# Stage two's rows and activations, and one key block in four of stage one, turned by VectorE and a trip through DRAM instead of TensorE

## What is computed

```python
# stage one, per block: q = layernorm(x), k = v = ctx, all [128, 1024]
qh = softmax(Wq @ q, over the 64 of a head) / 8      # 8 heads of 64
kh = softmax(Wk @ k, over the 1024 columns)
context = kh @ (Wv @ v).T                            # per head, 64 x 64
out = Wo @ (context.T @ qh) + bo
u = out / norm(out over the 128 channels) * g * sqrt(128)
x = x + tanh(g_xattn) * u
# stage two, per block: y = layernorm(x), rows of 1024
scores = y @ Wr.T                                    # 64 experts
G = softmax of the 16 largest scores, 0 elsewhere
h = y @ A.T                                          # 64 experts x rank 16 = 1024
x = x + tanh(g_ffn) * 2 * (h * G) @ B
```

## Time and profile before

| | |
|---|---|
| median of 3 runs | 959.66 us (959.61 to 959.68) |
| the profiled execution | 959.67 us, of which the span is 957.9 |
| TensorE matmuls | 932.2 us busy (97%), 5084 |
| TensorE weight loads | 800.5 us (84%) |
| VectorE | 704.0 us (73%) |
| ScalarE | 492.2 us (51%) |
| GpSimd | 469.5 us (49%) |
| DMA | 88.31 MB, mean 92 GB/s |
| granted clock | 0.994 of full |
| chain that ended last | PE 81%, DVE 10%, issue 5%, ACT, POOL and DMA 1% each |

### The profile page before, as it was taken

How to read it: one execution, slowest core, us unless ns; L and a number is a source line. 1 busy time by engine, 2 the same in 40 slices (tenths; PEclk the granted TensorE clock), 3 DMA queues, 4 the chain that set the end, 5 groups by cost and what they waited for, 6 DMA issues and landing times.

```text
span 957.9 us, 16074 instructions
## 1 busy us (share of the span) xinstructions
PE 932.2 (97%) x5084; PEld 800.5 (84%) x5084; DVE 704.0 (73%) x1532; ACT 492.2 (51%) x974; POOL 469.5 (49%) x323
## 2 busy tenths in 40 slices
PE   7899999999999999999999799999999999999998
PEld 5687887888888888888888699999999999999986
DVE  6888888888888888888888857766666666666521
ACT  4687786678768767876787634222222222222100
POOL 3775657678777877785787824222222111111100
PEclk9999999999999999999999999999999999999999
DMA  4226231231323113311312853121111111111001
GB/s 153 89 66 249 93 104 49 89 133 66 109 91 133 66 68 132 109 68 66 131 45 88 300 199 128 67 67 67 66 67 67 66 66 66 66 66 45 23 23 44
DMA packets 24805, 88.31 MB, mean 92 GB/s; under 512 B 3264, under 2 KB 3264, under 8 KB 24768
## 3 DMA queue, kind: packets, MB, share of 16 engines
q1 hardware_dynamic: 19296, 67.91, 19.9%
q0 software_dynamic: 5184, 19.40, 6.1%
q10 hardware_dynamic: 288, 0.52, 0.2%
HBM read 71.04 MB, written 16.78 MB: 92 GB/s over the span
## 4 chain that ended last, share of the span: by engine, by line
PE 81%; DVE 10%; issue 5%; ACT 1%; POOL 1%; DMA 1%; DVEq 0%; ACTq 0%; POOLq 0%
PE ps L61 22%; PE ps L63 22%; PE ps L62 22%; PE ps L1307 6%; PE ps L1298 4%; DVE qT_lo L909 3%; PE ps L1288 2%; PE ps L1402 1%; PE ps L1373 1%; DVE mt L933 1%; DVE ekT_lo L916 1%; DVE qmax L895 1%; DVE bn L831 1%; DVE kmax L889 1%; DVE qsum L900 1%
## 5 line engine op out<-in xcount | busy, mean ns | idle before, releaser
L471 POOL TENSOR_TENSOR rb<-u_in,rb 128x1024 f32<-128x1024 f32 x14 | 33.7, 2408 | 255.4 <-DVE rb L885 255.4
L400 POOL TENSOR_TENSOR qe<-qe,qrec 128x1024 f32<-128x1024 f32 x64 | 121.2, 1903 | 47.1 <-DVE qrec L903 47.1
L61 PE MATMUL ps<-aT_hi,yT_hi 128*128 128x448 f32 (+2 forms) x384 | 128.4, 334 | 5.4 <-issue 5.4
L63 PE MATMUL ps<-aT_lo,yT_hi 128*128 128x448 f32 (+2 forms) x384 | 126.6, 330 | 0.0
L62 PE MATMUL ps<-aT_hi,yT_lo 128*128 128x448 f32 (+2 forms) x384 | 126.5, 330 | 0.0
L909 DVE TENSOR_TENSOR qT_lo<-ps,qT_hi 128x512 fp32r<-128x512 f32 x128 | 82.4, 686 | 49.0 <-ACT qT_hi L628 48.5
L393 POOL TENSOR_TENSOR qhalf<-qe 128x512 f32<-128x512 f32 x64 | 82.2, 1284 | 64.8 <-ACT qe L620 61.8
L61 PE MATMUL ps<-bT_hi,hT_hi 128*128 128x512 f32 x256 | 102.6, 401 | 0.0
L63 PE MATMUL ps<-bT_lo,hT_hi 128*128 128x512 f32 x256 | 100.0, 391 | 0.0
L62 PE MATMUL ps<-bT_hi,hT_lo 128*128 128x512 f32 x256 | 99.8, 390 | 0.0
L700 ACT ACTIVATE hT_hi<-ps 128x512 fp32r<-128x512 f32 x32 | 19.1, 597 | 143.8 <-PE ps L1402 143.8
(11 more groups left out here) (155 smaller groups left out, 2397.5 us busy)
## 6 DMA issues: line engine op xcount, KB each, us to landing
x_in<-in_x SPq DMA_DIRECT2D x16, 512.0 KB, 4.4
ctx_in<-in_ctx SPq DMA_DIRECT2D x16, 512.0 KB, 4.9
ctxT_in<-in_ctxT SPq DMA_DIRECT2D x16, 512.0 KB, 3.4
ctxT_hi<-in_ctxT POOLq DMA_DIRECT2D x16, 512.0 KB, 3.8
u_scratch<-osb SPq DMA_DIRECT2D x16, 512.0 KB, 3.8
out<-res SPq DMA_DIRECT2D x16, 512.0 KB, 2.8
x<-in_x SPq DMA_DIRECT2D x15, 512.0 KB, 4.0
u_in<-u_scratch SPq DMA_DIRECT2D x14, 512.0 KB, 3.2
```

What stands on the lines that cost most here:

```text
L61: nc.tensor.matmul(psum, whi, mhi, start=start, stop=False)
L63: return nc.tensor.matmul(psum, whi, mlo, start=False, stop=stop)
L400: nc.gpsimd.tensor_tensor(v, v, w, ALU.mult).then_inc(q_norm, 1)
```

## The change

VectorE can turn 32x32 blocks in place (`nc.vector.transpose`). The rest of a 128x128 turn, the blocks' exchange, is made by a store of the tile to a DRAM scratch (`put_turned`, one DMA) and four loads of 32 partitions each, in runs of 256 elements (`take_moved`). Both are issued on SP, and SP waits for the store's end before it issues the loads.

- y of blocks 2 to 15: `turn_y` (VectorE, in place), trip, `y_raw`, then `hi_moved_y` and `lo_moved_y`, each one operation over 128x1024 from SBUF, in place of two from PSUM. `tr_y` stays for blocks 0 and 1.
- h of all 16 blocks: `turn_h` after the third `gated`, trip, `h_raw`, `hi_moved_h`, `lo_moved_h`. `down(b)` is one piece. Rows of A and B are laid out in another order to suit.
- Strip 0 of the keys in every body: `exp_k(b, 0)` writes in another order, `turn_k` follows on VectorE after `sum_q(b-1, 2)`, the trip ends in `osb`, then `hi_moved_k` (ScalarE) and `lo_moved_k` (GpSimd, after `mts`). `osb` must be free of block b-2's store, and `out_o(b-1, 0)` waits for `lo_moved_k(b)`.
- TensorE takes `tr_q(b-1, 2)` where `tr_k(b, 0)` stood; ScalarE takes `hi_q(b-1, 2)` ahead of `exp_k(b, 2)`. Stage two's `sum_u(b + 2)` moves behind `up(b, 0)`, `psN` to another bank.
- SP loads the raw A one block per body in bodies 2 to 9, not all eight ahead of body 2.

```diff
+        def put_turned(queue, place, src, s):
+            queue.dma_start(turn_dram[place], src).then_inc(s, 16)
+        def take_moved(queue, dst, place, s):
+            for q in range(P // 32):
+                queue.dma_start(dst[32 * q:32 * q + 32, :].rearrange("j (a f) -> j a f", f=256),
+                                turn_dram[place].rearrange("(a j) (q f) -> q j a f", a=P // 32, f=256)[q]).then_inc(s, 16)
...
+            def move_k(b):
+                wait_apart(sp, sp_turns, (k_turned, b + 1))
+                put_turned(sp, 2, ek[:, 0, :], k_put)
+                if not (isinstance(b, int) and b < 2):
+                    wait_apart(sp, sp_turns, (u_stored, 16 * (b - 1)))
+                wait_apart(sp, sp_turns, (k_put, PUT * (b + 1)))
+                take_moved(sp, osb, 2, k_moved)
...
                     load(ctx_in[:, :], ctx, b + 1, ctx_loaded)
+                    move_k(b)
...
+                if not isinstance(i, int) or b <= NB - 2:
+                    sp.wait_ge(y_turned, b)
+                    put_turned(sp, 0, y[(j + 2) % 2][:, :], y_put)
+                    sp.wait_ge(y_put, PUT * b)
+                    take_moved(sp, y_raw, 0, y_moved)
                 if not isinstance(i, int) or b <= NB - 4:
-                    sp.wait_ge(y_T, 2 * b + 4)
                     load_u(b + 3, j % 2)
+                sp.wait_ge(h_turned, b + 1)
+                put_turned(sp, 1, hg[:, :], h_put)
+                sp.wait_ge(h_put, PUT * (b + 1))
+                take_moved(sp, h_raw, 1, h_moved)
...
+            def lo_moved_k(b):
+                pool.wait_ge(k_hi, 8 * b + 2)
...
+            def hi_moved_k(b):
+                act.wait_ge(k_moved, MOVED * (b + 1))
...
+            def hi_moved_y(b):
+                act.wait_ge(h_mm, 3 * b)
+                act.wait_ge(y_moved, MOVED * (b - 1))
...
+            def hi_moved_h(b):
...
+                elif started(b):
+                    act.wait_ge(f_mm, 2 * b)
+                act.wait_ge(h_moved, MOVED * (b + 1))
...
                 if head:
-                    hi_k(b, 0)
+                    hi_moved_k(b)
+                if tail and head:
+                    hi_q(b - 1, 2)
+                if head:
                     exp_k(b, 2)
                     exp_q(b, 1)
-                if tail and head:
-                    hi_q(b - 1, 2)
...
                 b = SLOTS * i + j + 1
+                first = isinstance(i, int) and b == 1
+                if not first:
+                    hi_moved_h(b - 1)
                 if not isinstance(i, int) or b <= NB - 2:
                     normalise(b + 1, (j + 2) % SLOTS)
-                hi_h(b - 1, 1)
+                if first:
+                    hi_moved_h(0)
                 exp_scores(b)
                 if not isinstance(i, int) or b <= NB - 2:
-                    hi_y(b + 1)
-                hi_h(b, 0)
+                    hi_moved_y(b + 1)
...
                 if tail:
                     sum_q(b - 1, 2)
+                if head:
+                    turn_k(b)
...
                     max_q(b, 1)
                     max_k(b, 2)
-                    lo_k(b, 0)
...
-                if not (isinstance(i, int) and b < 2):
+                if not first:
                     result(b - 2, (j + 1) % 2, (j + 3) % SLOTS, 2 * i + (j - 1) // 2)
-                if not isinstance(i, int) or b <= NB - 3:
+                    lo_moved_h(b - 1)
+                if norms:
                     part_u(b + 2)
+                if ahead:
+                    turn_y(b + 1, j % 2)
                 route(b)
...
                     gated(b, p)
-                if not isinstance(i, int) or b <= NB - 2:
-                    lo_y(b + 1)
-                lo_h(b, 0)
-                if not isinstance(i, int) or b <= NB - 3:
+                turn_h(b)
+                if ahead:
+                    lo_moved_y(b + 1)
+                if norms:
                     stats2(b + 2, (j + 3) % SLOTS)
...
                 up(b, 0)
-                if isinstance(i, int) and b == 1:
-                    tr_h(0, 0)
-                else:
-                    tr_h(b - 1, 1)
+                if norms and not first:
+                    sum_u(b + 2)
                 up(b, 1)
-                if isinstance(i, int) and b == 1:
-                    tr_h(0, 1)
                 up(b, 2)
-                if not isinstance(i, int) or b <= NB - 3:
+                if first:
                     sum_u(b + 2)
-                if not isinstance(i, int) or b <= NB - 2:
-                    tr_y(b + 1, j % 2)
-                down(b - 1, 0)
-                tr_h(b, 0)
-                down(b - 1, 1)
+                down(b - 1)
```

More of the change, by code:

```diff
@@ L4, with flamingo_layer @@
 import math
-def flamingo_layer(nc, x, ctx, ctxT, g_xattn, g_ffn, WqT, WkT, Wv, WoT, bo, g, AT, BT, u_dram, out):
+def flamingo_layer(nc, x, ctx, ctxT, g_xattn, g_ffn, WqT, WkT, Wv, WoT, bo, g, AT, BT, u_dram, turn_dram, out):
     f32 = mybir.dt.float32
@@ L293, in _ @@
             sp.wait_ge(wq_low, 1)
-            for t in range(DC):
-                sp.dma_start(a_raw[:, t, :], AT[t]).then_inc(a_loaded, 16)
-            with sp.Fori(2, NB - 2) as b:
+            with sp.Fori(2, 2 + DC) as b:
+                sp.dma_start(a_raw[:, bass.ds(b - 2, 1), :].rearrange("p o n -> p (o n)"),
+                             AT[bass.ds(b - 2, 1)].rearrange("o p n -> (o p) n")).then_inc(a_loaded, 16)
+                body(b, head=True, tail=True, ahead=True)
+            with sp.Fori(2 + DC, NB - 2) as b:
                 body(b, head=True, tail=True, ahead=True)
@@ L910, in lo_q, with turn_k @@
                                             qT[0][:, :, v].bitcast(f32), ALU.subtract).then_inc(q_lo, 1)
+            def turn_k(b):
+                dve.wait_ge(k_exp, 4 * b + 1)
+                nc.vector.transpose(ek[:, 0, :], ek[:, 0, :]).then_inc(k_turned, 1)
             def lo_k(b, j):
@@ L1190, in _ @@
             gated(0, 2)
+            turn_h(0)
             lo_y(1)
@@ L1392, in up @@
                 last.then_inc(h_mm, 1)
-            def tr_h(b, g):
-                pe.wait_ge(hg_done, 3 * b + 2 + g)
-                if g == 1 or started(b):
-                    pe.wait_ge(h_lo, 2 * b + g)
-                else:
-                    pe.wait_ge(o_out, 2 * NB)
-                for n in range(4):
-                    w = (4 * g + n) * P
-                    last = nc.tensor.transpose(psG[:, n * P:n * P + P], hg[:, w:w + P], ident[:, :])
-                last.then_inc(h_T, 1)
@@ L1448, in body @@
                     mm_k(b, 2)
-                    tr_k(b, 0, next(turn))
                 if tail and head:
+                    tr_q(b - 1, 2, next(turn))
                     output(b - 1, 0, range(CH // 2))
@@ L1458, in body @@
                         up(0, 0)
-                    tr_q(b - 1, 2, next(turn))
-                    if not head:
+                        tr_q(b - 1, 2, next(turn))
                         output(b - 1, 0, range(CH))
@@ L1526, in _ @@
                 ffn_body(NB // SLOTS - 1, j)
-            tr_h(NB - 1, 1)
-            down(NB - 1, 0)
-            down(NB - 1, 1)
+            down(NB - 1)
 _INS = ["x", "ctx", "ctxT", "g_xattn", "g_ffn", "WqT", "WkT", "Wv", "WoT", "bo", "g", "AT", "BT"]
```

165 lines of the change are left out of this document (111 added, 54 removed).

## The result

The changed kernel takes **964.87 us** (six runs, 963.63 to 967.65), 1.0056 of the kernel before (interval 1.0041 to 1.0071): 5.2 us slower, where 957.0 was forecast. The profiled execution took 964.83 with a span of 962.8; the one of before had 957.9, so 4.9 are to be found.

What follows compares the result with a forecast made beforehand. TensorE was taken to bound stage two, with VectorE close behind in stage one. Stage two's -24.9 us was nearly offset by losses in stage one and at the seams: -2.6 in all, 957.0 us, range 950 to 967.

Steps and rivals of the forecast that it cites:

- the seam: Between the stages: `down(0)` about 4 us later behind the trip of h, plus 1.8 of lower clock; together +5.7 us.
- the gain of stage two: Stage two: TensorE sheds the `tr_h` and `tr_y` transposes, 1.8 us a block, their replacements hidden; -24.9 us together.
- bodies 2 to 4: Stage one, bodies with `part_early`: no idle time on VectorE, so the turn's 1.14 less 0.4, +0.76 each, 2.3 us.
- rival 4: Stage two: transposes go but blocks stay at 24.8 us, the path or VectorE becoming the bound; 981 us, chance 0.04.
- Body 0: Start of stage one: the key strip's trip has no cover and ScalarE waits for it; +6.3 us (4.9 to 10).
- The ten plain bodies: Stage one, bodies 1 and 5 to 13: `turn_k` delays VectorE's line 0.6 against 0.4 of slack; +0.23 each, 2.3 us.
- GpSimd: Stage one: added `lo_moved_k` of 2.4 us costs +2.4 in body 14, +2.2 in 15, +0.4 in the eight `lo_a` bodies.
- The end: End of stage two: `down(15)` waits a whole trip behind `up(15)`, +0.5, less block 15's 0.9 of transposes; -0.4 us.
- Rival 3: Stage one: the trip of k is late, 11.7 us, and every body pays 0.4; 967 us, chance 0.2.
- rival 1: Whole kernel: TensorE is the bound everywhere, stage one's 16 x 0.92 count too, seams cost nothing; 918 us, chance 0.05.
- rival 2: Stage one: the turn is hidden in VectorE's idle time, and GpSimd's added work too; 951 us, chance 0.15.
- the signs of being wrong: Four loads over 7 us, ScalarE waiting for them in every body, or stage-one bodies keeping their 32.9 us.

Runs made afterwards that it cites:

- no_turn: The changed kernel without VectorE's 32x32 turn of the key strip, which goes through DRAM unturned (not the reference's result): 950.04 us, ratio 0.9895 to the kernel before.
- two_turns: The changed kernel with the key strip turned twice on VectorE, which leaves it unturned (not the reference's result): 987.32 us, ratio 1.0291 to the kernel before.

## Why the prediction was wrong

The forecast was 2.6 us faster, and the kernel is 5.2 slower. The mechanisms were mostly right; the sizes of five terms were not, and four of these errors go one way. By size the steps that failed are the seam (+5.7), the gain of stage two (-24.9, which has the move of `sum_u` at nothing), bodies 2 to 4 (+2.3, without a word on the clock) and the way from body 15 to the landing of A (+2.2).

- **Stage two, -24.9**: the mechanism held. A block was to last 22.9 to 23.0 and lasts 23.06; y's and h's trips, SP's order and VectorE are hidden as costed, rival 4 did not happen. It is mis-sized by 2.5 over `up(3)` to `up(15)`: 1.5 is block 9, the rest 0.1 a block. I had costed the move of `sum_u` at nothing without asking what VectorE does ahead of it.
- **The seam, +5.7**: the wait before `down(0)` was forecast at 6 and measured 7.4, half clock behind it as said, but the cause was incomplete. I followed one chain to one consumer. That `down` was merged into one wait, that y(2) now stands behind `turn_h(1)`, and `sum_u(4)` behind the trip of h(1), were all in the diff; the step that failed is "what is late next", asked once instead of three times. It is 2.8 too small: `down(0)` came 5.8 later behind `up(1, 0)` (19.59, 13.76 before), not 4.1, and block 2 lost 0.8 more (23.87, with a wait of 0.6 for `part_u(4)`).
- **Body 0, +6.3**: right in mechanism and near in size (7.1; the trip 7.0, forecast 7.3). The lower clock behind the wait was not in it. What it missed is the lever: the turn waited 5 us in VectorE's order.
- **Bodies 2 to 4, +0.76 each**: measured +0.9 each without the clock, and 1.5 for the clock in one of them. That TensorE's wait for `qmax` there would double, and what such a wait does to its clock, I had not asked, though I had priced just that at `down(0)` from the earlier trace rows. In other executions of the same bodies the 1.5 came twice or not at all, so this part of the miss was luck.
- **The ten plain bodies, +0.23 each**: 0.07 each. The forecast let 0.53 of the turn's 1.14 be taken up by idle time and 0.4 by the removed transposes. By bodies 10 to 13 of `no_turn` the turn costs 0.3 of its 1.25, so the path took up 0.9, and the removed work gave 0.24. It is 1.6 too large, with the 0.4 of the `lo_a` bodies, which was nothing.
- **GpSimd, +2.4 and +2.2**: body 14 right (2.3, of which 1.5 went with the subtraction). Body 15 up to the casts of A came to 1.7, but relief on GpSimd alone did not take it back. Missed: the casts of A run closer ahead of B's loads, and A lands 1.9 later; that the one causes the other is not shown.
- **The end, -0.4**: 0.0, because `down(15)` waited 1.15 for `result(14)` behind `lo_moved_h(15)`.
- Rival 3, the nearest to the measured time, gave 967 by another mechanism than the one that acted; that the time landed inside the range, near its upper end, is luck as far as the mechanism goes: the reasons are spread over five terms. Two rivals' times do not follow from their own terms: rival 1 comes to 920 (959.7 - 24.9 - 14.7), not 918, and rival 2 to 950.1, not 951. No chance rests on that.
- Of the signs of being wrong two came in part: ScalarE waits for the loads in bodies 5 to 9, though not in all, and the plain bodies nearly keep their 32.9 (32.96).

The misses add up: 0.8 - 2.0 + 2.0 - 0.3 + 1.4 + 2.8 + 2.5 + 0.4 = 7.6, the 7.5 between -2.6 and +4.9. Six of eight have one sign: each edit was followed to its first consumer and no further.

## What to carry over

Taking work from the bounding engine pays only where that engine bounds: in stage two each block shed 1.7 of 1.8 us, in stage one the same edit could gain 0.24 a body at most and cost up to 7. Try the halves of such a change apart. A mean over bodies can hide two kinds of them: look at each. And at a seam follow the chain until nothing is late any more: a fix that removes the first of three limits measures as nothing, and is still needed.

## What was not expected of the hardware

- A TensorE wait of 1.9 to 2.3 us in an otherwise full stretch is followed by a spell at the lower clock in some executions and not in others, at 1.4 to 1.6 us each time. In full stretches nine waits of 1.5 to 1.6 (`two_turns`) and those of up to 1.1 were not; in body 0, with other waits just ahead, some of 1.2 and 1.3 were.
- A store of 512 KB and four loads behind it take 7.0 us in body 0 (DMA share 0.43), 10.8 beside other loads (0.67), and the store alone 7.9 with the casts of B in flight (367 GB/s, DMA share 1.00 from 592 to 600).
- A loop's back edge held VectorE for 2.95 to 3.67 us, with a DMA share of 0.02 at the time in the changed kernel, for 0.5 in the kernel before.
- VectorE's subtraction over two SBUF tiles takes 1.23, and 2.1 where GpSimd's operation was already running (611.23 above, in the seam; GpSimd's began at 609.86). In a steady block VectorE's begins first (752.56, GpSimd's at 752.66): it takes 1.23 and GpSimd's 3.4 instead of 2.4.
